# One stage for the return of the expert rows and the set-up of the graph layers, the far-sender table on ScalarE, the attention vectors in one pass per head

## The chip, the cores and the metric

The kernel runs on one core of a Trainium2 chip. The metric is the device time of one execution in microseconds (us), from the median of several runs. Engine names: PE is TensorE (PEld its weight loads), DVE is VectorE, ACT is ScalarE, POOL is GpSimd, SP is SyncE, which here only issues transfers. A name followed by q (PEq, POOLq, SPq) is that engine's sequencer.

## What is computed

There are N = 1250 nodes with D = 512 features each, and four layers, each of which adds its result to x. The change lies at the seam of the second and the third:

```python
x = x + _L0_gnn_ref(_layernorm(x), edge_attr_4, edge_attr_8, edge_index, ...)
x = x + _L0_ffn_ref(_layernorm(x)[None], ...)[0]        # experts, 2 of 4 groups, 2 of 8 in each
x = x + _L1_gnn_ref(_layernorm(x), edge_index, ...)     # two attention layers and a matrix
x = x + _L1_ffn_ref(_layernorm(x)[None], ...)[0]

def _L0_ffn_ref(inp, ...):          # per group g
    moe = moe + iw[:, e:e + 1] * (h @ W2[g, e] + b2[g, e])
    y = _layernorm(z + moe, gln_g[g], gln_b[g])
    out = out + gw[:, g:g + 1] * y

def gat_conv(x, src, dst, W, att_src, att_dst, bias):
    h = (x @ W).reshape(N, HEADS, HID)
    a_src, a_dst = jnp.sum(h * att_src, axis=-1), jnp.sum(h * att_dst, axis=-1)
    e = jax.nn.leaky_relu(a_src[src] + a_dst[dst], NEG_SLOPE)
    m = jax.ops.segment_max(e, dst, num_segments=N)
    e = jnp.exp(e - m[dst])
    ...
```

## The kernel before, in words

The nodes are cut into T = 10 tiles of P = 125. Work is staged: each `nc.Block()` is a stage with its own program on each engine, written out by hand with semaphores, and a stage begins when every engine has ended the one before (a barrier). There is no planner: an engine's order is the order of its lines.

**`routed_experts` (L1071)** has three stages. The first (planning, DVE above all) finds for each node its four experts, their gates (`wide`, `chosen_gate`) and the rows of `slot_rows` in which the results will lie (`slots`). POOL first clears `small` (L1183), then makes the constants on which DVE waits at L1225; SP loads the small tables and the first weights. The second stage runs 70 blocks of 128 rows through their experts and stores them to `slot_rows` in DRAM. The third (L1558 to L1690) is **the return**. POOL clears `wide_t` (L1562) and gathers, for every tile, four rows per node (`yg`, L1567; YB = 3 tiles deep). PE turns `wide` (L1584) and then for each tile makes `offsets` (L1593, two products), `sums` (L1600, L1601) and `gains` (L1608, two). On DVE `mix(t)` (L1644 to L1663) weighs and adds the rows and takes their statistics, `finish(t)` (L1670 to L1681) scales and adds them into `out`, which is x; the loop is `mix(t + 1)`, `finish(t)`. ACT takes the square roots (L1632). SP stores each finished tile (L1575).

**`graph_setup` (L1699)** is the next stage. On DVE it first normalises all ten tiles of x (`Norm`: L771, L774, L787, L791), and then for each tile subtracts two runs of the table `counts` (L1770), adds the identity (L1774) and writes `far` (L1776), which is -1e30 where a node sends to a receiver nothing and 0 elsewhere. Between tiles 2 to 5 it calls `attention_vectors` (L1818), which for each 128 rows of W1 and each of two attention rows makes a product of 128x1024 (L1824) and sums it by head (L1826). PE turns x (L1787) and `counts` (L1796, ten transposes a tile); ACT copies both out of PSUM (L1806, L1812).

**`graph_attention` (L1830)** follows twice. Its start needs `xt`, `wa`, `cnt` and `far`. In the first call `wa` is there; in the second DVE makes it with `attention_vectors`, eight times, while PE multiplies the first three tiles (L1954); PE then needs it at L1964. The pass for the maximum (L2093) is a product-and-reduce instruction over 1250 elements with an accumulator read behind it.

```python
mix(0)                                  # return, DVE
for t in range(T):
    if t + 1 < T:
        mix(t + 1)
    finish(t)
```

Of the kernel before, what the change touches and what calls it, by code (L numbers as in the profile page):

```python
# [4 lines left out]
F32 = mybir.dt.float32  # L5
F32R = mybir.dt.float32r
I32 = mybir.dt.int32
# [8 lines left out]
N = 1250  # L16
# [1043 lines left out]
J = TOP * TOP  # L1060
BLOCKS = (N * J + X * 127) // 128
# [9 lines left out]
def routed_experts(nc, queue, lg, z, weights, b2, gln_g, gln_b, z_rows, slot_rows, out, spare, x_new):  # L1071
# [8 lines left out]
    M = X + 2 * NG  # L1080
    ROWS = 128
    ctx = ExitStack()
    with ctx:
# [5 lines left out]

        chosen_gate = sb("chosen_gate", [P, J, T])  # L1090
        slots = sb("slots", [P, J, T], I32)
        wide = sb("wide", [P, T, TOP, M])
        ident = sb("ident", [128, 128])
        eps = sb("eps", [P, 1])
        small = sb("small", [ROWS, 3, D])
# [22 lines left out]
        with rooms:  # L1118
# [49 lines left out]
            with nc.Block() as block:  # L1168
                @block.sync
                def _(sp):  # L1170
                    sp.wait_ge(zeros, 1)
                    sp.dma_start(small[0:X, 0, :], b2.rearrange("g e d -> (g e) d")).then_inc(small_in, 16)
                    sp.dma_start(small[X:X + NG, 1, :], gln_g).then_inc(small_in, 16)
                    sp.dma_start(small[X + NG:M, 2, :], gln_b).then_inc(small_in, 16)
# [3 lines left out]
                    sp.wait_ge(small_in, 16 * 3)  # L1178
# [172 lines left out]
        with rooms:  # L1351
# [30 lines left out]
            with nc.Block() as block:  # L1382
                @block.sync
                def _(sp):
                    for e in range(X):
# [6 lines left out]
                        sp.sem_inc(ready, 1)  # L1392

                @block.gpsimd
                def _(pool):
# [143 lines left out]
        rooms = ExitStack()  # L1539
        with rooms:  # L1540
            def room(name, shape, dt=F32):
                return rooms.enter_context(nc.sbuf_tensor("p4_" + name, shape, dt))

            wide_t = room("wide_t", [ROWS, T * TOP, P])
            yg = room("yg", [P, YB, J, D])
            moe = room("moe", [P, 2, TOP, D])
            stats = room("stats", [P, 2, TOP, 6])
            mv = room("mv", [P, 2, TOP, 2])
            std = room("std", [P, 2, TOP])
            rstd = room("rstd", [P, 2, TOP])  # L1550
            psB, psG, psF = (ps[0:2], ps[2:4]), ps[4:6], ps[6:8]
            wide_mm, wide_ok, off_mm, moe_ok, sum_mm, gain_mm, scaled, out_ok, mv_ok, std_ok, kept = (sem(s) for s in (
                "wide_mm", "wide_ok", "off_mm", "moe_ok", "sum_mm", "gain_mm", "scaled", "out_ok", "mv_ok", "std_ok",
                "x_stored"))
            cleared = sem("cleared")
            back = queue["back"]
            CUT = 4 * P

            with nc.Block() as block:
                @block.gpsimd  # L1560
                def _(pool):
                    nc.gpsimd.memset(wide_t[:], 0.0).then_inc(cleared, 1)  # L1562
                    for t in range(T):
                        if t >= YB:
                            pool.wait_ge(moe_ok, t - YB + 1)
                        for j in range(J):
                            pool.indirect_dma_start(yg[:, t % YB, j, :], None, slot_rows,  # L1567
                                                    bass.IndirectOffsetOnAxis(ap=slots[:, j, t:t + 1], axis=0))\
                                .then_inc(back[t % YB], 16)

                @block.sync
                def _(sp):
                    for t in range(T):
                        sp.wait_ge(out_ok, t + 1)
                        sp.dma_start(x_new[t * P:(t + 1) * P, :], out[:, t, :]).then_inc(kept, 16)  # L1575
                    sp.wait_ge(kept, 16 * T)

                @block.tensor
                def _(pe):
                    for i in range(T * TOP // 4):  # L1580
                        if i >= 2:
                            pe.wait_ge(wide_ok, i - 1)
                        for c in range(4):
                            last = nc.tensor.transpose(psG[i % 2][0:M, c * P:(c + 1) * P],  # L1584
                                                       wide[:, (4 * i + c) // TOP, c % TOP, :], ident[0:P, 0:P])
                        last.then_inc(wide_mm, 1)
                    pe.wait_ge(wide_ok, T * TOP // 4)

                    def offsets(t):
                        if t >= 2:  # L1590
                            pe.wait_ge(moe_ok, t - 1)
                        for a in range(TOP):
# [1128 lines left out]
```

## Time and profile before

| | us |
|---|---|
| median of 3 runs | 2354.38 (2353.44 to 2356.39) |
| profiled execution, its own time | 2353.07 |
| its span, first to last instruction | 2351.4 |
| PE, DVE, ACT, POOL busy | 2003.0, 1513.0, 1118.3, 748.9 |
| mean granted clock of TensorE | 0.917 of full |

The profiled execution is the record of one run. Its rows give engine, source line, what is written and read, the number of instructions, and in brackets the idle time before them with what ended it. In windows each engine has its busy time and number of instructions; PEclk is the granted clock of TensorE as a share of 2.4 GHz, so 0.50 is 1.2 GHz. A product of f32 matrices shows as two MATMUL records. Ends of matmuls are modelled: where several follow one another the distance of their starts is the better measure.

### The profile page before, as it was taken

What the parts mean: (1) busy time and instruction counts of PE and PEld (TensorE: products, weight loads), DVE (VectorE), ACT (ScalarE), POOL (GpSimd) and SP (SyncE); (2) the same over time, 40 slices, a digit from 0 to 9 for tenths busy, and PEclk for the clock granted to TensorE, in tenths of its full rate; (3) what the DMA queues carried; (4) which work ended last, traced back from release to release, by engine and by line L of the source; (5) the groups of instructions that cost most, each with busy time, mean ns of one, the idle gap of its engine ahead of it and who ended that gap; (6) DMA issues with size and microseconds to landing.
All of it is one profiled execution on the core that took longest, in us unless ns stands there. A gap on an engine that the chain in (4) does not pass through costs nothing. (4 is left out here: it accounts for less than half of the span.)

```text
span 2351.4 us, 36494 instructions
## 1 busy us (share of the span) xinstructions
PE 2003.0 (85%) x11260; PEld 1288.4 (55%) x11261; DVE 1513.0 (64%) x2331; ACT 1118.3 (48%) x2278; POOL 748.9 (32%) x629
## 2 busy tenths in 40 slices
PE   5899999999997738999975497999999999980997
PEld 2444444444445727777732444777344777540997
DVE  1289999999995774333348865777763778428011
ACT  5777777777773404555510313666001676210332
POOL 4287777777770012444453000000000000000453
PEclk9989999999998957999988598999999999995998
DMA  5565555555551423788544313000012100221794
GB/s 160 168 170 157 154 155 154 153 154 152 155 155 53 95 85 129 268 261 265 174 129 132 96 43 115 22 22 1 18 43 81 64 22 1 104 100 46 221 277 94
DMA packets 200741, 285.12 MB, mean 121 GB/s; under 512 B 116698, under 2 KB 128677, under 8 KB 196543
## 3 DMA queue, kind: packets, MB, share of 16 engines
q0 software_dynamic: 98272, 142.08, 21.2%
q1 hardware_dynamic: 100158, 137.67, 19.0%
q10 hardware_dynamic: 2209, 4.07, 0.5%
q8 instruction: 56, 0.92, 0.2%
q14 instruction: 46, 0.38, 0.0%
HBM read 233.52 MB, written 49.84 MB: 121 GB/s over the span
## 5 line engine op out<-in xcount | busy, mean ns | idle before, releaser
L565 POOL DMA_INDIRECT p_s<-node_table,e_src_rows x320 | 454.5, 1420 | 147.4 <-issue 86.7
L2004 PE MATMUL g_psO<-g_h,g_ring 125*125 125x257 f32 x1600 | 372.4, 388 | 19.7 <-DVE g_ring L2136 10.3
L2004 PEld LDWEIGHTS g_psO<-g_h,g_ring 125*125 125x125 f32 x1600 | 296.6, 190 | 92.1 <-DVE g_stage L2130 26.6
L703 PE MATMUL p_psW<-e_w,p_hid 64*125 64x512 f32 x640 | 275.4, 654 | 50.2 <-ACT z L580 24.7
L622 DVE TENSOR_TENSOR g_b<-z,p_s 125x1536 f32<-125x1536 f32 x160 | 273.6, 1751 | 0.0
L711 PE MATMUL p_psM<-g_b 125*32 125x384 f32 x648 | 249.5, 533 | 11.0 <-DVE p_key L684 5.9
L580 ACT ACTIVATE z<-p_psW 125x512 f32<-125x512 f32 x320 | 187.2, 585 | 147.0 <-PE p_psW L703 139.0
L715 PE MATMUL p_psM<-g_b 125*32 125x256 f32 x648 | 218.8, 422 | 0.0
L714 PE MATMUL p_psM<-g_b 125*32 125x256 f32 x648 | 211.3, 410 | 0.0
L713 PE MATMUL p_psM<-g_b 125*32 125x256 f32 x648 | 193.8, 426 | 0.0
L585 ACT ACTIVATE p_of<-e_node_ids,z 125x314 bf16<-125x314 f16 x320 | 176.2, 551 | 6.8 <-PE p_psC L720 3.1
L2069 ACT ACTIVATE g_ring<-g_ring,g_ident 125x625 f32<-125x625 f32 x160 | 131.0, 819 | 85.3 <-DVE g_ring L2117 84.5
L703 PEld LDWEIGHTS p_psW<-e_w,p_hid 64*125 64x125 f32 x640 | 71.6, 185 | 181.2 <-ACT z L580 113.8
L2136 DVE SCALAR_TENSOR_TENSOR g_ring<-g_ring,g_cnt 125x625 f32<-125x625 f32 x160 | 128.7, 804 | 39.2 <-ACT g_ring L2069 39.1
L1954 PE MATMUL g_psO<-g_a,g_b 128*125 128x512 f32 x320 | 141.2, 603 | 2.1 <-PEq L1907 2.1
L2093 DVE CUSTOM_DVE_ANT_0 g_ring<-g_rb,g_far 125x1250 f32<-125x1250 f32 x80 | 110.7, 1453 | 49.7 <-DMA g_rb<-sender_rows 49.7
L60 POOL MEMSET p_ident<- 128x128 f32 x5 | 1.0, 206 | 434.2 <-POOLq L2669 368.1
L1438 PE MATMUL p_ps<-p_xt,p_first_own 128*128 128x128 f32 x1120 | 138.4, 277 | 0.0
L1399 POOL DMA_INDIRECT p_xg<-z_rows,p_node_at x70 | 71.1, 1016 | 210.8 <-DVE p_y L1535 154.4
L712 PE MATMUL p_psM<-g_b 125*32 125x128 f32 x648 | 135.9, 294 | 0.0
L1438 PEld LDWEIGHTS p_ps<-p_xt,p_first_own 128*128 128x128 f32 x1120 | 132.6, 194 | 0.5 <-issue 0.5
L1450 PE MATMUL p_ps<-p_second_own,p_ht 128*128 128x512 f32 x280 | 131.6, 593 | 0.0
(357 smaller groups left out, 3775.2 us busy)
## 6 DMA issues: line engine op xcount, KB each, us to landing
p_ring<-in_L_ffn_weights SPq DMA_DIRECT2D x32, 1025.0 KB
slot_rows<-p_y POOLq DMA_DIRECT2D x70, 256.0 KB
p_w1s<-in_L_ffn_w SPq DMA_DIRECT2D x16, 1024.0 KB
g_a<-in_L_ffn_w SPq DMA_DIRECT2D x16, 1024.0 KB
hidden<-g_b SPq DMA_DIRECT2D x40, 250.0 KB, 3.2
p_hid<-hidden SPq DMA_DIRECT2D x160, 62.5 KB
g_rb<-receiver_rows SPq DMA_DIRECT2D x16, 610.4 KB
p_s<-node_table,e_src_rows POOLq DMA_INDIRECT x320
```

Source lines behind the costliest of these rows:

```text
L565: pool.indirect_dma_start(s[:, g % 4, c, :, :].rearrange("p k u -> p (k u)"), None, node_table, bass.IndirectOffsetOnAxis(ap=src_rows[:, g ...
L580: nc.scalar.activation(w[:, b, c, :, :].rearrange("p k u -> p (k u)"), psW[c % 2][0:P, :], ACT.Copy).then_inc(w_ok, 1)
L585: nc.scalar.activation(of[:, b, c, :], node_ids[:], ACT.Sigmoid, scale=STEEP, bias=rise[:, bass.ds(g, 1), c:c + 1].rearrange("p o c -> p ( ...
L622: last = nc.vector.tensor_tensor(msg[:, b, :, q:q + 3, :], w[:, b, :, p:p + 1, :].broadcast_to([P, C, 3, MUL]), s[:, at, :, 1:4, :], ALU.mult)
L703: nc.tensor.matmul(psW[c % 2][0:P, :], hid[part, b, c // 2, :], w4[part, :], start=True, stop=True)\
L711: nc.tensor.matmul(psM[i][0:32, 0:3 * MUL], a, rows_[:, 0:3, :], start=begin, stop=end)
L713: nc.tensor.matmul(psM[i][64:96, 0:2 * MUL], own[1], rows_[:, 4:7:2, :], start=begin, stop=end)
L714: nc.tensor.matmul(psM[i][32:64, MUL:3 * MUL], own[0], rows_[:, 4:6, :], start=False, stop=end)
L715: last = nc.tensor.matmul(psM[i][96:128, 0:2 * MUL], own[2], rows_[:, 4:8:3, :], start=begin, stop=end)
L1438: last = nc.tensor.matmul(psH[u % 2][:, m * 128:(m + 1) * 128], w1s[u % 2][:, k, m * 128:(m + 1) * 128], xt[:, u % 2, k, :], start=k == 0, ...
L1954: last = nc.tensor.matmul(psO[0:P, 2 * (t % 2) + j, :], xt[:, k, t * P:(t + 1) * P], ws[:, k, j * 512:(j + 1) * 512], start=k == 0, stop=k ...
L2004: last = nc.tensor.matmul(psO[0:P, j, 0:HW], ring[:, i % RING, j * P:(j + 1) * P], h[:, s, hd, :], start=s == 0, stop=s == T - 1)
```

## The change

The third stage of `routed_experts` and `graph_setup` go, and one stage, `combine`, stands in their place. What the return needs from the planning lies in a free part of the room `g_b` (`for_combine`), so that it outlives `routed_experts`. In `combine` each tile goes through return, normalisation, turning and the difference of the counts before the next: the DVE loop is `mix(t + 1)`, `finish(t)` with the row statistics, `difference(t + 2)`, attention vectors (tiles 2 to 5), `norm(t)`. `psB`, `psF` and `psX` have one buffer where they had two, `psC` has two banks where it had six, `rows16` three buffers where it had two. `far` is written by ACT as relu(-1e30 * counts + 1e30), positive, and subtracted at the maximum. `attention_vectors` uses four product-and-reduce instructions of 256 elements with an accumulator read each, in place of one product and one reduction of 1024; this holds in both attention layers. `small` is cleared and loaded during the experts' blocks, not before planning. `wide_t` is no longer cleared.

```diff
 # routed_experts, planning
-                    nc.gpsimd.memset(small[:], 0.0).then_inc(zeros, 1)
-                    pool.wait_ge(zeros, 1)
                     identity(nc, pool, tick, ident[:])
...
 # routed_experts, blocks, POOL
                     for b in range(XB - 1):
                         gather(b)
+                    nc.gpsimd.memset(small, 0.0).then_inc(zeros, 1)
...
 # combine
+            def _(sp):
+                for t in range(RB):
+                    counts_in(t)
+                for i, row in enumerate((att_src, att_dst)):
+                    sp.dma_start(att[:, i, :], row.partition_broadcast(128)).then_inc(att_in, 16)
+                for k in range(KD):
+                    sp.dma_start(ws[:, k, :], w[k * 128:(k + 1) * 128, :]).then_inc(ws_in[k], 16)
+                for t in range(T):
+                    if t + RB < T:
+                        counts_in(t + RB)
+                    sp.wait_ge(out_ok, t + 1)
+                    sp.dma_start(x_new[t * P:(t + 1) * P, :], xs[:, t, :]).then_inc(kept, 16)
...
+                def offsets(t):
+                    pe.wait_ge(wide_ok, t * TOP // 4 + 1)
+                    if t:
+                        pe.wait_ge(moe_ok, t)
...
+                def sums(t):
+                    if t:
+                        pe.wait_ge(out_ok, t)
...
+                def gains(t):
+                    pe.wait_ge(wide_ok, TURNS)
+                    if t:
+                        pe.wait_ge(scaled, t)
...
+                def turn_counts(t):
+                    pe.wait_ge(looped, t + 1)
+                    for k, (a, b) in enumerate(PARTS):
+                        n = NPARTS * t + k
+                        if n >= 2:
+                            pe.wait_ge(cnt_ok, n - 1)
...
+                for t in range(T):
+                    sums(t)
+                    gains(t)
+                    if t + 2 < T:
+                        offsets(t + 2)
+                    if t:
+                        turn_rows(t - 1)
+                    if t + 2 < T:
+                        turn_counts(t + 2)
+                turn_rows(T - 1)
...
+                def take_counts(t):
+                    act.wait_ge(looped, t + 1)
+                    nc.scalar.activation(far[:, t, :], rows[:, t % 2, 0:N], ACT.Relu, bias=away[:], scale=FAR)\
+                      .then_inc(far_ok, 1)
...
+                for t in range(T):
+                    if t + 1 < T:
+                        roots(t + 1)
+                    row_root(t)
+                    if t:
+                        take_rows(t - 1)
+                    if t + 2 < T:
+                        take_counts(t + 2)
...
+                difference(0)
+                difference(1)
+                mix(0)
                 for t in range(T):
+                    if t + 1 < T:
+                        mix(t + 1)
+                    finish(t)
+                    if t + 2 < T:
+                        difference(t + 2)
+                    if 2 <= t < 2 + KD:
+                        v.wait_ge(att_in, 32)
+                        v.wait_ge(ws_in[t - 2], 16)
+                        attention_vectors(nc, v, wa_ok, ws, att, prod, wa, t - 2)
+                    norm(t)
...
 # attention_vectors
-        n = tick(nc.vector.tensor_tensor(prod[:, i, :], ws[:, k, :], att[:, i, :], ALU.mult))
-        tick.wait(n)
-        nc.vector.tensor_reduce(wa[:, k, i, :], prod[:, i, :].rearrange("p (h c) -> p h c", h=HEADS),
-                                AX.X, ALU.add).then_inc(wa_ok, 1)
+        for hd in range(HEADS):
+            own = slice(hd * HC_GAT, (hd + 1) * HC_GAT)
+            last = nc.vector.tensor_tensor_reduce(out=prod[:, i, own], in0=ws[:, k, own], in1=att[:, i, own], scale=1.0,
+                                                  scalar=0.0, op0=ALU.mult, op1=ALU.add, accum_out=wa[:, k, i, hd:hd + 1])
+        last.then_inc(wa_ok, 1)
```

The order of DVE before, in the middle of `graph_setup`: one tile's difference and far table (L1770 to L1776) between two calls of `attention_vectors`.

```order
L1824 TENSOR_TENSOR p_prod<-g_a,p_att 128x1024
L1826 TENSOR_REDUCE g_wa<-p_prod 128x4
L1770 TENSOR_TENSOR p_rows<-p_rows 125x1252
L1774 TENSOR_TENSOR p_rows<-p_rows,p_ident 125x125
L1776 TENSOR_SCALAR g_far<-p_rows 125x1250
```

And the order of DVE now, one round of the loop in `combine` behind its `mix(7)` (t = 6, without attention vectors): `finish(6)` from L1818, its row statistics (L1832, L1834), `difference(8)` (L1780, L1784), `norm(6)`. `p_moe` are the weighed rows, `g_b` holds x.

```order
L1818 SCALAR_TENSOR_TENSOR p_moe<-p_moe,p_mv,p_psG 125x512 x2
L1822 RECIPROCAL p_rstd<-p_std 125x2
L1826 SCALAR_TENSOR_TENSOR g_b<-p_moe,p_rstd,p_psF 125x512
L1829 SCALAR_TENSOR_TENSOR g_b<-p_moe,p_rstd,g_b 125x512
L1832 BN_STATS p_row_stats<-g_b 125x6
L1834 BN_AGGR p_row_mv<-p_row_stats 125x2
L1780 TENSOR_TENSOR p_rows<-p_rows 125x1252
L1784 TENSOR_TENSOR p_rows<-p_rows,p_ident 125x125
L1838 RECIPROCAL p_row_rstd<-p_row_std 125x1
L1842 TENSOR_SCALAR p_normed<-g_b,p_row_mv,p_row_rstd 125x512
```

The far table has left this engine, and the difference and the normalisation now stand between one tile's return and the next.

The order of PE before, at the end of the return and in all of `graph_setup`: the last tiles' `offsets` (L1593), `sums`, `gains`, then all the transposes.

```order
L1600 MATMUL p_ps<-g_b,p_ident 125x512
L1601 MATMUL p_ps<-p_small,p_wide_t 125x512
L1608 MATMUL p_ps<-p_small,p_wide_t 125x512 x2
L1559 UNCONDITIONAL_BRANCH
L1779 UNCONDITIONAL_BRANCH
L1787 MATMUL p_psX<-p_ident,g_b 128x125 x40
L1796 MATMUL p_psC<-p_ident,p_rows 125x125 x100
```

And the order of PE now, from the end of one round of the loop in `combine` through the next.

```order
L1698 MATMUL p_psC<-p_ident,p_rows 125x125 x10
L1669 MATMUL p_psF<-g_b,p_ident 125x512
L1670 MATMUL p_psF<-g_b,p_wide_t 125x512
L1678 MATMUL p_psG<-g_b,p_wide_t 125x512 x2
L1662 MATMUL p_psB<-g_b,p_wide_t 125x512 x2
L1687 MATMUL p_psX<-p_ident,p_normed 128x125 x4
```

The transposes of the counts (L1698) now stand ahead of the sums and the gains (L1669 to L1678) of the next tile, for which DVE waits in `finish`.

## Rows read from the trace of the kernel before

**Rows 1.** The page's head.
```profile
span 2351.4 us, 36494 instructions
```

**Rows 2.** Windows: from:to, length, busy per engine, PEclk, DMA share, GB/s.
```profile
1208.60:1284.70 76.10, 53.15 (x111) 20.73 (x109) 70.32 (x130) 2.96 (x10) 43.35 (x34) 0.95 0.51 150
1284.70:1289.70 5.00, 0.00 (x0) 0.00 (x0) 0.00 (x0) 0.00 (x0) 0.02 (x1) 0.50 0.17 51
1289.70:1350.30 60.60, 27.77 (x134) 23.85 (x135) 55.40 (x77) 18.16 (x38) 0.52 (x3) 0.58 0.34 104
1350.30:1353.60 3.30, 1.62 (x9) 1.36 (x9) 0.00 (x0) 1.34 (x3) 0.07 (x1) 0.50 0.00 0
```

**Rows 3.** Timeline of DVE, one tile of the return: start, us, instruction.
```profile
1221.91 1.41 DVE L1644 SCALAR_TENSOR_TENSOR p_moe<-p_yg,p_chosen_gate,p_ps 125x512 f32<-125x512 f32 x2
1225.96 1.39 DVE L1670 SCALAR_TENSOR_TENSOR p_moe<-p_moe,p_mv,p_ps 125x512 f32<-125x512 f32 x2
1229.13 1.41 DVE L1644 SCALAR_TENSOR_TENSOR p_moe<-p_yg,p_chosen_gate,p_ps 125x512 f32<-125x512 f32 x2
```

**Rows 4.** Timeline of DVE in graph_setup, difference, far, attention vectors.
```profile
1313.29 1.45 DVE L1770 TENSOR_TENSOR p_rows<-p_rows 125x1252 f32<-125x1252 uint16 x1
1315.11 0.81 DVE L1776 TENSOR_SCALAR g_far<-p_rows 125x1250 bf16<-125x1250 f32 x1
1315.83 1.22 DVE L1824 TENSOR_TENSOR p_prod<-g_a,p_att 128x1024 f32<-128x1024 f32 x1
1318.22 1.22 DVE L1824 TENSOR_TENSOR p_prod<-g_a,p_att 128x1024 f32<-128x1024 f32 x1
```

**Rows 5.** Timeline of DVE in the first attention layer, product-and-reduce.
```profile
1374.26 1.46 DVE L2093 CUSTOM_DVE_ANT_0 g_ring<-g_rb,g_far 125x1250 f32<-125x1250 f32 x1
1375.64 1.46 DVE L2093 CUSTOM_DVE_ANT_0 g_ring<-g_rb,g_far 125x1250 f32<-125x1250 f32 x1
```

**Rows 6.** Groups of instructions by line in 1280 to 1560 us.
```profile
L2136 DVE SCALAR_TENSOR_TENSOR g_ring<-g_ring,g_cnt 125x625 f32<-125x625 f32 x46 | 37.0, 804 | 9.2 <-ACT g_ring L2069 9.2
L2117 DVE SCALAR_TENSOR_TENSOR g_ring<-g_rb,g_as_low,g_lines 125x625 f32<-125x625 f32 x24 | 20.9, 870 | 27.0 <-ACT g_lines L2059 18.7 <-PE g_psO L2004 8.1
```

**Rows 7.** Groups of instructions by line in 1189 to 1354 us.
```profile
L1562 POOL MEMSET p_wide_t<- 128x2500 f32 x1 | 2.2, 2182 | 5.3 <-POOLq L1382 5.3
L771 DVE BATCH_NORM_STATS2 p_norm_stats<-g_b 125x6 f32<-125x512 f32 x10 | 6.0, 678 | 5.1 <-PEq L2664 5.1
L791 DVE TENSOR_SCALAR g_b<-g_b,p_norm_mv,p_norm_rstd 125x512 f32<-125x512 f32 x10 | 4.7, 543 | 0.0
L1812 ACT ACTIVATE g_cnt<-p_psC 125x500 uint16<-125x500 f32 (+1 forms) x30 | 13.3, 524 | 33.6 <-PE p_psC L1796 33.6
```

**Rows 8.** Waits: engine line <- releaser: us in total, times, longest.
```profile
DVE p_moe L1644 <- DMA p_yg<-slot_rows,p_slots: 20.5, 2, 18.5
SPq L1559 <- DMA x<-g_b: 3.6, 1, 3.6
```

**Rows 9.** Timeline of PE in the return and in graph_setup.
```profile
1223.47 1.88 PE L1593 MATMUL p_ps<-p_small,p_wide_t 128*125 128x512 f32 x4
1315.13 2.46 PE L1796 MATMUL p_psC<-p_ident,p_rows 125*125 125x125 f32 x10 [7.24 <-DVE p_rows L1774]
```

**Rows 10.** Windows of 4 us, columns as in Rows 2.
```profile
1220.00:1224.00 4.00, 3.82 (x6) 1.77 (x7) 3.80 (x8) 0.00 (x0) 3.09 (x4) 0.60 0.64 179
1304.00:1308.00 4.00, 3.74 (x31) 3.14 (x29) 2.78 (x4) 3.15 (x7) 0.00 (x0) 1.00 0.33 132
1312.00:1316.00 4.00, 0.87 (x4) 0.88 (x5) 3.90 (x6) 0.00 (x0) 0.00 (x0) 0.50 0.11 30
```

**Rows 11.** Timeline of ACT, a copy of 1024 elements.
```profile
1169.54 1.06 ACT L1492 ACTIVATE p_second_own<-p_ring 128x1024 f32 x1
```

**Rows 12.** Timeline of DVE in the planning stage.
```profile
850.59 3.49 DVE L1225 TENSOR_TENSOR p_ties<-p_ties,p_earlier 125x3200 f32<-125x3200 f32 x1 [1.97 <-POOL p_nodes L1206]
```

**Rows 13.** Timeline of PE in the second attention layer.
```profile
1698.42 16.95 PE L1964 MATMUL g_psX<-g_b,g_wa 128*8 128x512 f32 x48
```

More of the change, by code:

```diff
@@ L1060 @@
 J = TOP * TOP
+WIDE = X + 2 * NG
 BLOCKS = (N * J + X * 127) // 128
@@ L1068, with for_combine, routed_experts @@
 SLOTS = BLOCKS * 128
-def routed_experts(nc, queue, lg, z, weights, b2, gln_g, gln_b, z_rows, slot_rows, out, spare, x_new):
+def for_combine(spare):
+    at = X * X + 2 * J * T * X + T * (NG + 1) * NE
+    sizes = [T * TOP * WIDE, J * T, J * T]
+    parts = []
+    for size in sizes:
+        parts.append(spare[0:P, at:at + size])
+        at += size
+    return (parts[0].rearrange("p (t a m) -> p t a m", t=T, a=TOP), parts[1].rearrange("p (j t) -> p j t", j=J),
+            parts[2].bitcast(I32).rearrange("p (j t) -> p j t", j=J),
+            spare[0:WIDE, 0:3 * D].rearrange("p (k d) -> p k d", k=3))
+def routed_experts(nc, queue, lg, z, weights, b2, gln_g, gln_b, z_rows, slot_rows, out, spare):
     H = 256
@@ L1696, with combine @@
 TH = T // 2
-def graph_setup(nc, xs, counts, xt, cnt, far, w, ws, att_src, att_dst, wa):
+def combine(nc, queue, spare, xs, slot_rows, x_new, counts, xt, cnt, far, w, ws, att_src, att_dst, wa):
     ctx = ExitStack()
@@ L1750, in _ @@
                 tick(nc.gpsimd.memset(eps[:], EPS))
+                tick(nc.gpsimd.memset(away[:], -FAR))
+                for t in range(T):
+                    if t >= YB:
+                        pool.wait_ge(moe_ok, t - YB + 1)
+                    for j in range(J):
+                        pool.indirect_dma_start(yg[:, t % YB, j, :], None, slot_rows,
+                                                bass.IndirectOffsetOnAxis(ap=slots[:, j, t:t + 1], axis=0))\
+                            .then_inc(back[t % YB], 16)
@@ L1752, in _ @@
             @block.vector
             def _(v):
[L1754 to L1765 removed]
+                tick = Ticks(v, sem("mixed"))
@@ new lines, in finish @@
+                def finish(t):
+                    s = t % 2
+                    v.wait_ge(gain_mm, t + 1)
+                    v.wait_ge(mv_ok, t + 1)
+                    for a in range(TOP):
+                        last = nc.vector.scalar_tensor_tensor(moe[:, s, a, :], moe[:, s, a, :], mv[:, s, a, 0:1],
+                                                              psG[0:P, a, :], ALU.subtract, ALU.mult)
+                    last.then_inc(scaled, 1)
+                    v.wait_ge(std_ok, t + 1)
+                    r = tick(nc.vector.reciprocal(rstd[:, s, :], std[:, s, :]))
+                    tick.wait(r)
+                    v.wait_ge(scaled, t + 1)
+                    v.wait_ge(sum_mm, t + 1)
+                    m = tick(nc.vector.scalar_tensor_tensor(xs[:, t, :], moe[:, s, 0, :], rstd[:, s, 0:1],
+                                                            psF[0:P, :], ALU.mult, ALU.add))
+                    tick.wait(m)
+                    nc.vector.scalar_tensor_tensor(xs[:, t, :], moe[:, s, 1, :], rstd[:, s, 1:2], xs[:, t, :],
+                                                   ALU.mult, ALU.add).then_inc(out_ok, 1)
+                    v.wait_ge(out_ok, t + 1)
+                    n = tick(nc.vector.bn_stats(row_stats[:, t, :], xs[:, t, :]))
+                    tick.wait(n)
+                    nc.vector.bn_aggr(row_mv[:, t, :], row_stats[:, t, :]).then_inc(row_mv_ok, 1)
@@ L2156, in graph_layers @@
           nc.sbuf_tensor("g_wa", [128, KL, 2, HEADS], F32) as wa):
-        graph_setup(nc, view(b, T, D)[0:P], counts, view(a, KD, N), cnt, far, w1, view(a, KD, DH, at=KD * N), as1, ad1, wa[:, 0:KD, :, :])
+        combine(nc, queue, spare, view(b, T, D)[0:P], slot_rows, x, counts, view(a, KD, N), cnt, far, w1,
+                view(a, KD, DH, at=KD * N), as1, ad1, wa[:, 0:KD, :, :])
         with nc.sbuf_tensor("g_h", [P, T, HEADS, HW], F32) as h:
```

394 lines of the change are left out of this document (166 added, 228 removed).

## The prediction

> **What bounds the kernel now.** I read the stages by window first. The return ends at 1284.7 us, nothing runs for 5.0, `graph_setup` has DVE until 1350.3, and 3.3 later the first attention layer begins [rows 2]. In the return DVE is busy 70.3 of 76.1, in `graph_setup` 55.4 of 60.6 [rows 2]. So DVE is the bound of the whole stretch of 145.0 us, and what counts is DVE's work, the idle stretch between the stages, and the waits that the new order gives DVE. The waits say what starts the stretch: the first tile's gathers, for which DVE waits 18.5, and 2.0 more for the second [rows 8]. The timelines then give the price of each piece.
>
> **What goes.** The gap of 5.0 [rows 2], of which 3.6 is the wait for the last store of x [rows 8]. It moves behind work: the last store now goes out while the last tile is normalised and turned, which takes longer than 3.6. The rest of that gap, 5.0 - 3.6 = 1.4, holds the end of `routed_experts` with its clearing of semaphores; I put 1.0 of it at the one boundary that is left. Far goes from DVE: 1315.83 - 1315.11 = 0.72 a tile, 7.2 in all [rows 4]. Two of the ten differences now run in the wait for the first gathers, 1315.11 - 1313.29 = 1.82 each [rows 4], 3.6 together. In planning DVE waits 1.97 for POOL's constants [rows 12], and POOL starts with a clearing of 1536 columns; at the pace of `wide_t`, 2500 in 2.18 [rows 7], that is 1.35 less for DVE to wait. I take -1.4.
>
> **The attention vectors.** One product and one reduction of 1024 take 1318.22 - 1315.83 = 2.39 [rows 4], eight times 19.1. Now there are 32 short product-and-reduce instructions. The long one has a pitch of 1375.64 - 1374.26 = 1.38 for 1250 elements, with its accumulator read in it [rows 5]. At 0.96 elements a ns, which the bare 1250 / 1.30 would need, some 0.08 is fixed, so one of 256 takes 0.27 + 0.08 = 0.35, and 32 take 11.1. Bounds: 0.28 by proportion (9.0), 0.50 if its fixed part doesn't overlap (16). I take 11.1, since the long ones did overlap. Both sources are f32 here, where the row's far table is bf16. The nearest pair for that is a three-operand instruction with two f32 sources in SBUF, 870 ns for 625 elements, against one with an f32 and a uint16 source, 804 [rows 6]: 8% more, not twice. The Trainium skill, "Vector Engine (DVE) Microarchitecture Reference", section "Points that are easy to get wrong", says that the scalar-tensor-tensor shape with two non-bf16 SBUF sources halves throughput; by that a short one would take about 0.61, and the saving here would be gone.
>
> In the second attention layer the same edit is worth nothing: PE goes from the first three tiles into the product with `wa` with no idle time [rows 13], so it and not DVE sets that start. The cover is those three tiles; it is gone only if the 64 short instructions take longer than the 16 pairs, 38.2, that is over 0.60 each.
>
> **The new stage, DVE from the first mix.**
> - Start. Before, POOL cleared `wide_t` for 2.18 [rows 7] ahead of the first gather; now it makes the constants, some 0.7. With 1.0 for the boundary the gathers start 0.5 earlier: 1208.6 becomes 1208. Now 3.9 MB of counts, attention rows and W1 are asked for in the same moments. I add 1 here and 2 at the second tile. (The sizes are the code's: three tiles of counts at 0.31, two rows to 128 partitions at 0.52, W1 at 2.1.) Bounds: 0 if the queues don't disturb each other; +14 if these bytes went wholly ahead, since 179 GB/s at a share of 0.64 [rows 10] mean some 280 at most.
> - Mix and finish: 1229.13 - 1221.91 = 7.22 a tile [rows 3], 72.2.
> - Row statistics and their aggregation, now one by one behind the row that they need: 0.68 [rows 7] and 0.2, 9.0 for ten tiles.
> - Normalisation: 0.54 [rows 7] and a reciprocal of one column, 0.75 a tile, 7.5.
> - Eight differences at 1.82 [rows 4]: 14.5. Attention vectors: 11.1. **DVE's work is 114.3.**
>
> **What DVE waits for now.** The gathers of the second tile, 1.9 as before and 2 more: 4. In the last two tiles the root on ACT and the last `gains` have nothing before them: 2.3.
>
> The new wait is for `gains`. PE turns the counts of tile t + 2 ahead of `sums` and `gains` of tile t + 1, and can't start before DVE's difference. From its end: at full clock ten transposes take half of 2.46 [rows 9], but their third part needs a bank that ACT empties behind the far table. That is 1250 elements on ACT, 1.3 by 1.06 for 1024 [rows 11], and 0.52 for the copy [rows 7], so PE is done after 2.2. Four passes take at most 1.88 at full clock [rows 9], sums and gains together 3.5. So `gains` stand 5.7 after the difference. DVE needs them after normalisation (0.75) and `mix` (1225.96 - 1221.91 = 4.05 [rows 3]), at 4.8. That is 0.9 of wait in the four counted tiles without attention vectors; in the other four the vectors (2.8) cover it. At half clock the same path is 2.6 + 7.0 = 9.6, a wait of 4.8, and 2.0 behind the vectors. So 3.6 in all at full clock, 27 at half. What clock? PE has 6 products of 512 and 14 transposes a tile, 5.2 + 1.7 of 12 to 13.5, nearly 60%; the return had 0.95 of clock at 53.2 of 76.1, `graph_setup` 0.58 at 27.8 of 60.6 [rows 2]. This lies between, nearer the first, and a low clock makes PE denser. In the return too it was down once, 0.60 from 1220 to 1224 [rows 10], and came back. I take **6**.
>
> Transposes count for the clock here: from 1304 to 1308 PE did nothing else and had 1.00, while the short bursts from 1312 had 0.50 [rows 10]. The Trainium skill, "TensorE: Matmul & The Clock Gate", "Part 4: PE-mode transpose", says that the full clock does not engage for transposes. The trace disagrees with that; were it so, the fourteen transposes would count as idle, and the third rival would be likelier.
>
> - Tail: four transposes, one copy of 500 elements on ACT (0.5 [rows 7]) and the barrier, 2.2 (3.3 before [rows 2]).
>
> **The sum.** 1209 + 114.3 + 4 + 2.3 + 6 + 2.2 = 1337.8, against 1353.6: -15.8. With planning -1.4 the profiled execution goes from 2353.07 to 2335.9; its span of 2351.4 [rows 1] lies 1.7 below its time, both move alike. The median is 1.3 higher, so I predict **2337** for it. As a check from the other side: 4.0 of the gap, 7.2 of far, 3.6 of differences, 8.0 of vectors, 1.1 of tail and 5.2 of DVE's idle time in `graph_setup` (60.6 - 55.4) go, 29.1; 6 for `gains`, 3 for gathers and some 4 for instructions that now run one by one come, which leaves 16.
>
> **Rivals.**
> 1. *The gathers starve.* The transfers for the set-up sit on SP's queue beside the gathers. If those get a third of the DMA for the 3.9 MB, the first tile comes 4 later and the second 5 more than I took: some 2343. For it: 3.9 MB are 14 us of a full DMA, and the return alone took 0.51 of it [rows 2]. Against: POOL itself issues no faster than it did, and the first mix needs only 1 MB. Chance 0.12.
> 2. *Short product-and-reduce instructions are slow.* At 0.61 each, the 32 cost 19.5 instead of 11.1, +8.4, and the 64 in the second layer 39.0 against 38.2, +1: 2346. Against it the pair of rows 6. At 0.70 the whole gain would be gone. Chance 0.13.
> 3. *The clock stays low, and PE's order becomes the bound.* This ends slower. The cycle is then difference, counts, sums, gains (9.6), `finish` (1229.13 - 1225.96 = 3.17), statistics 0.9, difference 1.8: 15.5 a tile, 124 for eight, where I have 12.1 four times and 13.5 four times, 102; +22, and 3 more in each of the last two: 2365. It decides from about 0.6 of the stage at half clock. For it: `graph_setup` sat at 0.50 with a third of PE busy. Against: at 15.5 PE would be busy nine tenths, which released the clock wherever it happened. Chance 0.06.
> 4. *All waits are covered*, the gathers undisturbed, the clock full: 6 + 3 less, some 2328. Chance 0.12.
>
> **How the numbers follow.** My forecast, 2331 to 2343, has 0.57. A measurement of this kernel tells 0.2%, 4.7 us, from no change: faster means below 2349.7. Rival 2 reaches that only at its worst, rival 3 never. Faster 0.89, same 0.05, slower 0.06. The range for 8 in 10 goes from rival 4 to rival 2 and over it: 2326 to 2348.
>
> **What would show it.** In the changed profile: one idle stretch between the experts' blocks and the attention layer; its end about 16 earlier; far on ACT at 1.3; short product-and-reduce pitch near 0.35; DVE waiting for `gains` about 1 to 2 in tiles 1, 2, 7, 8 and hardly in 3 to 6; PEclk over 0.85; PE at the second layer's `wa` with no idle time. I am wrong if DVE idles over 15 in the stage, or if the pitch is over 0.5.

## The result, and the profile after

The changed kernel takes **2371.45 us**, median of 4 runs (2367.52 to 2372.42), against 2354.41 for the kernel before (4 runs): ratio 1.0079, 95% interval 1.0063 to 1.0094. It is slower by 0.8%, where 0.7% faster was forecast, and it lies outside the range. The profiled execution took 2367.52.

The page's head and clock row, after. The slices are 59 us each; the new stage lies in slices 21 to 23, where PE is 5, 8 and 8 tenths busy and its clock at 6, 6 and 5 tenths.
```profile
span 2365.7 us, 36678 instructions
PE   5898999999996839999958897999999999990997
PEclk9989999999998857999966598999999999995998
```

I count from the end of the experts' last block, 1190.08 before and 1189.71 after, to the first PE row of the attention layer. That **stretch** took 1353.57 - 1190.08 = 163.5 before [rows 2] and 1365.08 - 1189.71 = 175.4 after. Windows of after: from the first mix to the last, from there to DVE's end, the tail, and the start of the attention layer.
```profile
1220.31:1337.47 117.16, 95.13 (x211) 45.62 (x212) 96.42 (x224) 31.61 (x57) 33.66 (x28) 0.60 0.40 113
1337.47:1362.83 25.36, 18.72 (x33) 7.60 (x32) 13.27 (x27) 4.04 (x9) 0.00 (x0) 0.50 0.05 16
1362.83:1365.08 2.25, 1.09 (x5) 0.74 (x5) 0.00 (x0) 0.59 (x1) 0.04 (x1) 0.50 0.17 64
1365.08:1384.99 19.91, 19.91 (x53) 6.92 (x54) 0.00 (x1) 2.84 (x6) 0.60 (x4) 0.89 0.11 36
```
DVE's work is what was forecast: in the 142.5 us from the first mix to its end its waits sum to 30 (20.4 for `gains`, 8.7 for the second tile's gathers, 1.1 for small ones), which leaves 112 with the short gaps between instructions, where 114.3 was forecast. PE is busy 95 of 117 at a clock of 0.60, where the return had 0.95 [rows 2]. The rest is waits. DVE's in the stage, after (compare [rows 8]):
```profile
DVE p_moe L1818 <- PE p_psG L1678: 20.4, 6, 5.4
DVE p_moe L1792 <- DMA p_yg<-slot_rows,g_b: 18.5, 2, 9.8
DVE p_rows L1780 <- DMA p_rows<-counts: 17.3, 2, 11.9
```
The first row is the wait for `gains`. The other two are the start: the counts and gathers of the first tiles. The DMA view from 1189.71 to 1225 us, after (last number: us from issue to landing), and of before from 1190 to 1215:
```profile
q1 hardware_dynamic: 1216, 3.96, 42.3%
q0 software_dynamic: 2331, 2.90, 36.3%
g_a<-in_L_gnn_W SPq DMA_DIRECT2D x4, 512.0 KB, 26.1
p_yg<-slot_rows,g_b POOLq DMA_INDIRECT x14, 15.6
```
```profile
q0 software_dynamic: 2209, 2.66, 36.5%
p_yg<-slot_rows,p_slots POOLq DMA_INDIRECT x11, 4.4
```
And the window over the worst of it, after: a DMA share above one, all engines full.
```profile
1200.00:1220.00 20.00, 6.84 (x26) 3.67 (x24) 3.50 (x4) 5.58 (x8) 14.27 (x11) 0.59 1.05 251
```
POOL issues the gathers as early as forecast (first constants at 1196.35), but a gather lands after 15.6 us instead of 4.4. The first mix comes 30.6 us behind the experts' end, before it was 18.5. The Trainium skill, "DMA: Bandwidth & Descriptors", section "Queues, rings and completion order", says that each DMA engine takes turns between the queues that have work for it; the two shares above, 42 and 36%, fit that, but no run here shows the turns themselves.

How `gains` come late is seen on PE. Rows of its timeline, after: from the counts to `gains` in one tile, and the same for the last `gains`.
```profile
1323.73 2.67 PE L1698 MATMUL p_psC<-p_ident,p_rows 125*125 125x125 f32 x10 [2.23 <-DVE p_rows L1784]
1326.19 1.92 PE L1669 MATMUL p_psF<-g_b,p_ident 125*125 125x512 f32 x2
1328.04 1.33 PE L1670 MATMUL p_psF<-g_b,p_wide_t 40*125 40x512 f32 x2
1329.20 1.88 PE L1678 MATMUL p_psG<-g_b,p_wide_t 40*125 40x512 f32 x4
1336.88 2.66 PE L1698 MATMUL p_psC<-p_ident,p_rows 125*125 125x125 f32 x10 [2.31 <-DVE p_rows L1784]
1339.34 1.91 PE L1669 MATMUL p_psF<-g_b,p_ident 125*125 125x512 f32 x2
1341.18 2.07 PE L1670 MATMUL p_psF<-g_b,p_wide_t 40*125 40x512 f32 x2
1343.05 3.61 PE L1678 MATMUL p_psG<-g_b,p_wide_t 40*125 40x512 f32 x4
```
From the end of DVE's difference to the end of `gains` it is 7.4 in the first and 9.8 in the second, which runs wholly at half clock (forecast: 5.7 at full, 9.6 at half). DVE's side:
```profile
1331.12 1.41 DVE L1818 SCALAR_TENSOR_TENSOR p_moe<-p_moe,p_mv,p_psG 125x512 f32<-125x512 f32 x2 [2.67 <-PE p_psG L1678]
1346.70 1.41 DVE L1818 SCALAR_TENSOR_TENSOR p_moe<-p_moe,p_mv,p_psG 125x512 f32<-125x512 f32 x2 [5.09 <-PE p_psG L1678]
```
What stays odd is the clock: PE is busy 81% of the time here, and in the return 70% went with 0.95 [rows 2]. One thing about its products is new, and the description of the change doesn't name it: `small` and `wide_t` are 40 rows deep (the rows over which a product sums) and no longer 128.

### The profile page after: what moved, and what is told of

It reads as the page before. It is cut to its first block and busy times, and to the rows that moved or that the text cites. A ratio compares the mean times of both kernels' runs of the same rounds, so it can differ in the third digit from the quotient of the medians.

```text
span 2365.7 us, 36678 instructions
## 1 busy us (share of the span) xinstructions
PE 2038.6 (86%) x11260; PEld 1300.8 (55%) x11261; DVE 1484.0 (63%) x2474; ACT 1134.3 (48%) x2297; POOL 752.7 (32%) x629
## 5 line engine op out<-in xcount | busy, mean ns | idle before, releaser
L565 POOL DMA_INDIRECT p_s<-node_table,e_src_rows x320 | 459.8, 1437 | 141.9 <-issue 88.8
L580 ACT ACTIVATE z<-p_psW 125x512 f32<-125x512 f32 x320 | 187.1, 585 | 147.7 <-PE p_psW L703 135.5
L715 PE MATMUL p_psM<-g_b 125*32 125x256 f32 x648 | 221.6, 427 | 0.0
L714 PE MATMUL p_psM<-g_b 125*32 125x256 f32 x648 | 213.3, 414 | 0.0
L713 PE MATMUL p_psM<-g_b 125*32 125x256 f32 x648 | 196.4, 431 | 0.0
```

The source lines that it names most:

```text
L565: pool.indirect_dma_start(s[:, g % 4, c, :, :].rearrange("p k u -> p (k u)"), None, node_table, bass.IndirectOffsetOnAxis(ap=src_rows[:, g ...
L580: nc.scalar.activation(w[:, b, c, :, :].rearrange("p k u -> p (k u)"), psW[c % 2][0:P, :], ACT.Copy).then_inc(w_ok, 1)
L713: nc.tensor.matmul(psM[i][64:96, 0:2 * MUL], own[1], rows_[:, 4:7:2, :], start=begin, stop=end)
L714: nc.tensor.matmul(psM[i][32:64, MUL:3 * MUL], own[0], rows_[:, 4:6, :], start=False, stop=end)
L715: last = nc.tensor.matmul(psM[i][96:128, 0:2 * MUL], own[2], rows_[:, 4:8:3, :], start=begin, stop=end)
```

## The experiments

The theories. **K**: the start is late because 3.9 MB for the set-up fill the DMA engines. **G**: `gains` are late because PE turns the counts ahead of them. **R**: the products of 40 rows hold the clock down. Rival to R, **P**: the pattern of dense and idle moments in the new order does it. All ran in four groups (1 to 4, 5 to 8, 9 to 12, 13 and 14), each with its own runs of the kernel before (medians 2344.3 to 2352.7), so only ratios compare. A ratio is the time over that of the kernel before. "+26.6" is a time behind the end of the experts' last block; before, the first mix is at +18.5 and the second at +24.6, and in the change at +30.6 and +43.5. The clock is that from the first mix to the last. Stretch, waits and clock come from one profiled execution each.

**1 (e1_late). Attention rows and W1 later.**
```
 for t in range(T):
     if t + RB < T: counts_in(t + RB)
+    if t == 0:
+        sp.wait_ge(moe_ok, 2)
+        ...the att and ws transfers, which stood ahead of the loop
```


> The changed kernel, but SP asks for the attention rows and W1 (3.1 MB) only once the second tile's rows have been weighed (moe_ok 2), not at the start of the stage. Theory K: the two first waits for gathers (9.8 and 8.7 us in the changed kernel, first mix at 1220.3 and not at 1208) come from these transfers standing beside the gathers. Then the first mix starts near 1209, the second waits 2 to 4, and the whole is 12 to 16 us below the changed kernel (about 2356). Rival: the gathers are late for a reason of their own (rows not yet stored, POOL slower), then both waits stay and the time stays within 3 us of 2371.

Measured: 2349.09, ratio 1.0024 (1.0014 to 1.0033), stretch 167.7. First mix at +26.6, where about +19 was expected, second at +33.3 instead of +43.5. K holds, for a third of the first mix's delay and half of the second's: 1.2 MB of counts still travel beside the gathers, which land after 6.9.

**2 (e2_order). PE's order.** 
```
-turn_counts(1)
 for t in range(T):
     sums(t)
     gains(t)
+    if t + 1 < T: turn_counts(t + 1)
     if t + 2 < T: offsets(t + 2)
     if t: turn_rows(t - 1)
-    if t + 2 < T: turn_counts(t + 2)
```

> The changed kernel with one edit on PE: the counts of a tile are turned behind the next sums and gains, not ahead of them. Theory G: the 20.4 us that DVE waits for gains come from this order at a low clock. Then they fall to 6 to 9 (the last tile's 5.4 stays, since nothing stands before it), and the time falls by 11 to 14, to about 2358. Rival: PE is simply full at half clock (13.9 us a tile), so that the wait only moves to the offsets or the counts: less than 4 us.

Measured: 2347.15, ratio 1.0008 (0.9996 to 1.0020), stretch 166.1. The waits for `gains` halve, 20.4 to 10.5, a little less than expected; PE is busy 108 of 115 and its clock is 0.56. So G holds. That PE is busier doesn't bring the clock, which speaks against P as long as the products are 40 deep.

**3 (e3_rows). Products 128 rows deep again.** 
```
-wide_t = sb("wide_t", [WIDE, T * TOP, P])
+wide_t = sb("wide_t", [128, T * TOP, P])
-spare[0:WIDE, 0:3 * D]          # small
+spare[0:128, 0:3 * D]
+nc.vector.memset(wide_t[:], 0.0).then_inc(cleared, 1)
```

> The changed kernel, but the products with wide_t and small are 128 rows deep again (the lower rows zero, cleared by DVE in its first wait) and not 40. Theory R: TensorE's granted clock fell (0.62 in the stage at 0.82 busy, where the return before had 0.95 at 0.70) because products 40 rows deep count for less. Then PEclk in the stage is over 0.85, the waits for gains fall from 20.4 to under 9, and the time falls by 12 or more. Theory P: the clock fell because of the order of work (transposes and idle stretches), then PEclk stays near 0.6 and the time within 3 us.

Measured: 2352.76, ratio 1.0031 (1.0021 to 1.0042), stretch 170.0. The order of work is the change's; DVE clears `wide_t` (2.1 us) in its first wait. Windows from the first mix to the last, in this kernel, then in experiment 2:
```profile
1213.60:1331.29 117.69, 80.19 (x211) 43.99 (x212) 96.75 (x224) 31.42 (x57) 33.72 (x28) 0.76 0.40 113
```
```profile
1211.22:1326.28 115.06, 108.03 (x205) 46.89 (x206) 96.45 (x225) 30.14 (x55) 33.67 (x28) 0.56 0.41 115
```
PE is less busy than in 2 and has more clock, 0.76. Depth counts, but the result lies between the two expectations: over 0.85, waits for `gains` under 9 and 12 us off were expected of R, and the waits are 14.9 and the stretch is 5.4 shorter. Experiments 10 and 11 show that the order of work has a share too.

**4 (e4_before40). The kernel before with products 40 rows deep**, nothing else, in `offsets`, `sums` and `gains`:
```
-wide_t[0:ROWS, TOP * t + a, :], small[0:ROWS, 1, :]
+wide_t[0:M, TOP * t + a, :], small[0:M, 1, :]
```

> The kernel before with one edit: its products in the return are 40 rows deep and not 128 (the same numbers, the lower rows were zero). Theory R: PEclk in the return falls from 0.95 to near 0.5 to 0.6, PE needs 10.4 us a tile at half clock where DVE needs 7.2, and the kernel gets 15 to 30 us slower. Theory P: PEclk stays at 0.95 and the time within 2 us of before.

Measured: 2372.41, ratio **1.0115** (1.0098 to 1.0132), the stretch 192.7 instead of 163.5. Its return, first mix to last, then the same window of the kernel before, then two rows of its PE:
```profile
1199.97:1287.52 87.55, 87.55 (x99) 28.96 (x97) 61.07 (x112) 2.66 (x9) 40.73 (x34) 0.50 0.44 124
```
```profile
1208.60:1272.49 63.89, 47.61 (x103) 18.92 (x102) 60.32 (x112) 2.66 (x9) 43.35 (x34) 0.97 0.59 170
```
```profile
1239.72 1.06 PE L1608 MATMUL p_ps<-p_small,p_wide_t 40*125 40x512 f32 x1
1240.58 3.62 PE L1593 MATMUL p_ps<-p_small,p_wide_t 40*125 40x512 f32 x4
```
PE never idles in 87.55 us, and the granted clock is 0.50 throughout. The same products with 88 rows of zeros below them had 0.97. R is shown, in the old order, with no transpose in that window: five of six products (512 columns, two records each) are 40 deep, one of six 125.

**5 (e5_all). The three edits together.**

> The changed kernel with three edits at once: attention rows and W1 asked for only after the second moe tile is ready; PE turns the counts of a tile behind the next sums; the products 128 rows deep. Alone each took 7.7, 9.3 and 5.4 us off the changed kernel's stretch from the experts' end to the attention layer's first PE row (175.4 to 167.7, 166.1, 170.0). Theory A (three separate causes: full DMA, order of PE's queue, clock held low by shallow products): they add, stretch 153 to 156, ratio to before 0.995 to 0.997. Theory B (one cause, the waits for the gains, which each edit shortens and which only go once): the gain stops where DVE has no wait for gains left, stretch 158 to 164, ratio 0.998 to 1.001. In both the first mix stays about 26 us behind the experts' end, since the counts' 1.2 MB are still asked for beside the gathers.

Measured: **2330.09**, ratio **0.9936** (0.9922 to 0.9949), stretch 147.1. Window from the first mix to the last, and DVE's waits:
```profile
1206.16:1307.01 100.85, 72.13 (x216) 36.03 (x217) 96.13 (x224) 31.05 (x57) 34.45 (x29) 0.90 0.54 151
```
```profile
DVE p_moe L1795 <- DMA p_yg<-slot_rows,g_b: 7.5, 1, 7.5
DVE p_moe L1821 <- PE p_psG L1681: 4.0, 1, 4.0
```
The first mix is at +25.7. Stretch and ratio lie below what A allowed, and B falls: the clock went up to 0.90, and the waits for `gains` sank to one. But that the three together give more than their sum is not shown. The stretch is 28.3 less than in the change's first profile, where the three alone gave 7.7, 9.3 and 5.4, 22.4 in all; against its second profile (177.3, experiment 12) it is 30.2 less, and the three alone make 28.1. By the ratios, with 1.0074 for the change, the three alone took 0.50, 0.66 and 0.43%, 1.59 in all, and together 1.38.

**6 (e6_start). The counts only after the first tile's gathers**, and DVE's first mix ahead of its first difference. On top of 5:
```
+sp.wait_ge(back[0], 16 * J)
 for t in range(RB): counts_in(t)
...
-difference(0)
-difference(1)
 mix(0)
+difference(0)
```
PE, ACT and DVE then take the counts one tile later throughout.

> As e5_all, and the counts are asked for only after the first tile's gathers have landed; DVE does the first mix ahead of the first difference. Theory A (the lost 12 us at the start are the gathers' turn in full DMA engines): first mix at +18.5 to +20 as in the kernel before (+18.5) instead of +26 to +31, the gathers' median time to landing back at 5 to 6 us, and the stretch 5 to 8 us shorter than in e5_all; ratio to before 0.991 to 0.995. Rival (it is queue issue on POOL or the cleanup ahead of them that is late, not the engines being full): first mix stays above +24.

Measured: 2335.4, ratio 0.9950 (0.9935 to 0.9966), stretch 150.6. The first mix is at +18.5, as before the change: K is shown for it; the gathers land after 6.0. But the stretch doesn't fall, it is 3.5 longer than in 5. DVE waits 15.0 for gathers where 5 has 7.5, the second mix is at +28.6, 3.7 ahead of 5 and no longer 7.2, and the clock is 0.83.

**7 (e7_oldvec). Attention vectors as before**, in both layers.
```
-for hd in range(HEADS): ... tensor_tensor_reduce(out=prod[:, i, own], ...)
+nc.vector.tensor_tensor(prod[:, i, :], ws[:, k, :], att[:, i, :], ALU.mult).then_inc(pr_ok, 1)
+v.wait_ge(pr_ok, 2 * k + i + 1)
+nc.vector.tensor_reduce(wa[:, k, i, :], ..., AX.X, ALU.add).then_inc(wa_ok, 1)
```

> The changed kernel with the attention vectors as before (a product of the whole row, then a reduction, with a wait between) in both graph layers. If they lie on the path, DVE's work in the stage grows by 16 passes of about 1.2 us against 32 of 0.345: 8 us longer, ratio about 1.011 to 1.012. If half the tiles that carry them wait for gains from PE anyway, part of it is hidden: 3 to 6 us longer, ratio 1.009 to 1.010. The second graph layer stays as it is within 0.5 us (its vectors are covered).

Measured: 2363.72, ratio 1.0077 (1.0059 to 1.0094), stretch 183.7, 8.4 longer than in the change's first profile. The time is not what either case expected. The change's second profile is in experiment 12.

**8 (e8_fardve). The far table by DVE.**
```
-nc.scalar.activation(far[:, t, :], rows[:, t % 2, 0:N], ACT.Relu, bias=away[:], scale=FAR)
+v.wait_ge(looped, t + 1)
+nc.vector.tensor_scalar(far[:, t, :], rows[:, t % 2, 0:N], 0.0, CAP, ALU.is_equal, ALU.mult)
```

> The changed kernel with the far-sender table again by DVE (tensor_scalar, eq and times a cap) and not by ScalarE. Theory A (DVE's own work bounds the stage): 10 passes of about 0.7 us more on DVE, 7 us longer, ratio about 1.011. Theory B (while PE's clock is low the chain PE, ACT, PE behind the gains bounds it, so DVE has room): within 2 us of the changed kernel, ratio 1.007 to 1.009, DVE's waits for gains shorter by what its own work grew.

Measured: 2360.93, ratio 1.0072 (1.0055 to 1.0090), stretch 177.1; DVE's busy time from first to last mix rises from 96.4 to 103.0, its waits for `gains` sink from 20.4 to 14.3. What ScalarE takes over was, in the changed kernel, given back as waiting: B.

**9 (e9_sep). The kernel before, stages apart, with only the far table by ScalarE and the new vectors.** The edits of 7 and 8 the other way round, in `graph_setup`; ScalarE takes far(t) ahead of the copies of tile t.

> The kernel before, its two stages left apart, with only the two other parts of the change: far-sender table by ScalarE and attention vectors in one pass per head. In the setup of the graph layers they take 16 passes of 1.22 us off DVE for 32 of 0.345 (8.5 us) and 10 of 0.81 us (8.1, the last of which was beside PE's transposes). If DVE alone bounds that part: 15 to 16 us shorter, stretch 148, ratio 0.993 to 0.994. If in the six tiles without attention vectors the counts (two buffers, 1.0 us of wait in two tiles before), PE at half clock (2.5 us a tile) and ScalarE (1.33 + 1.34 us a tile) take over: 11 to 13 us shorter, stretch 151 to 153, ratio 0.9945 to 0.9955. Either would say that the joining itself brings nothing beyond these two parts.

Measured: 2341.09, ratio **0.9959** (0.9945 to 0.9973), stretch 152.2, the second of the two cases. ScalarE's copies now wait 7.0 for PE and PE 13.9 for DVE in the set-up. Two of the three parts of the change are worth 0.4%; the third, the joining as it was made, costs 1.0074 / 0.9959, about 1.2%.

**10 (e10_late_rows) and 11 (e11_order_rows). Two of the three edits of 5**: late transfers and deep products (10), order and deep products (11).

> Of e5_all's three edits only two: the late attention rows and W1, and products 128 rows deep; PE keeps the changed kernel's order. Additive from the single runs: stretch 175.4 - 7.7 - 5.4 = 162, ratio about 1.000. If the clock is what multiplies them (it was 0.60 and 0.76 with one edit, 0.90 with three), it stands at 0.8 or more between first and last mix and the stretch is 153 to 158, ratio 0.996 to 0.998.

> Of e5_all's three edits only two: PE's counts behind the next sums, and products 128 rows deep; attention rows and W1 are asked for at the stage's start as in the change, so first and second mix stay at +30 and +44. Additive: stretch 175.4 - 9.3 - 5.4 = 160.7, ratio about 0.999. If the clock multiplies them: clock 0.85 or more, stretch 155 to 158, ratio 0.996 to 0.998.

Measured: 10: 2347.76, ratio 0.9987 (0.9977 to 0.9997), stretch 159.9, clock 0.76. 11: 2346.75, ratio 0.9985 (0.9973 to 0.9996), stretch 157.9, clock 0.86. The stretches lie 2 to 3 below the sums; against the change's second profile the sums are 160.4 and 158.8, and they lie only 0.5 and 0.9 below; the ratios show nothing of it. So 10 is in effect additive, and its clock stayed under the 0.8 of the other case; 11 reached the clock and the stretch of the other case, but not its ratio. With products 128 deep the order of the change has 0.76 (3 and 10) and the new order 0.86, so P has a share beside R. Only order and depth together bring the clock over 0.8. The rest of the waits for `gains` is then 4.4, against 16.8 in 10.

**12 (after_again). The changed kernel again.**

> The changed kernel on the chip of the experiments, as their base: ratio to before 1.005 to 1.008, stretch 174 to 177, clock about 0.60 between first and last mix.

Measured: 2367.84, ratio 1.0074 (1.0056 to 1.0091), stretch 177.3, clock 0.60. So the slowdown is found again. Against it, 7 and 8 are the same within their intervals. Their stretches say +6.5 and -0.2, but one execution each, and the change's own two differ by 1.9. So in the changed kernel the far table by ScalarE shows no gain, and whether the new vectors are worth something there stays open.

**13 (e12_one) and 14 (e13_spread). The start once more.** 13 asks for only the first tile's counts at once; 14 also spreads W1's four pieces over three tiles. On top of 5:
```
+counts_in(0)
+sp.wait_ge(back[0], 16 * J)
-for t in range(RB): counts_in(t)
+for t in range(1, RB): counts_in(t)
...
 difference(0)
-difference(1)
 mix(0)
+difference(1)
```

> e5_all, with only the first tile's counts asked for at the stage's start and the others once the first tile's gathers have landed; DVE's second difference moved behind the first mix. If the late start is a term of its own: first mix at +19 to +20, stretch 142 to 146, ratio 0.991 to 0.992. If the wait comes back at the second tile's gathers (beside which the counts now travel) or in a lower clock: stretch 148 to 151, ratio 0.993 to 0.994.

> e12_one, with W1's four pieces asked for one tile after the other (from the second tile on) and not together. If the gathers of the second and third tiles waited for W1's 2 MB: 2 to 4 us shorter than e12_one, wait for gathers under 5 us in all. If not: within 1 us of it.

Measured: 13: 2337.63, ratio 0.9934 (0.9915 to 0.9953), stretch 150.4, first mix +18.7. 14: 2335.53, ratio 0.9931 (0.9909 to 0.9953), stretch 145.9 in its profile, which its time doesn't bear out. None is told apart from 5. Waits of 13:
```profile
DVE p_rows L1785 <- DMA p_rows<-counts: 11.7, 3, 5.9
DVE p_moe L1797 <- DMA p_yg<-slot_rows,g_b: 6.1, 2, 5.0
DVE p_moe L1823 <- PE p_psG L1683: 4.4, 1, 4.4
```
The wait goes from the first tile's gathers to the second tile's counts. In 5, 13 and 14 DVE waits 20 to 25 us in all for the cleanup, counts and gathers; the order of the transfers shifts that between them and hardly lessens it.

The best versions, 5, 13 and 14, are faster than both kernels, by 0.65% against before and 1.4% against the change.

## Why the prediction was wrong

Two steps failed: the gathers at the start were priced by POOL's pace and not by full DMA engines, and the clock was taken from PE's share of busy time, without the new depth of its products. By its own sign, DVE idle over 15 in the stage, it was wrong: 30 us of waits from the first mix on. By its steps, in the profiled execution, forecast start of the attention layer 1337.8, measured 1365.1, 27.3 later:

- **The start failed**: "I add 1 here and 2 at the second tile". The first mix came at 1220.3, not 1209: **+11.3**. The wait of the second tile was 8.7, not 4: **+4.7**. The bound of +14 was worked out and then not believed; I argued from POOL's pace of issue, while the engines, full, set the pace of landing. Experiments 1 and 6 show it. Rival 1 was this mechanism and had 0.12, at half its size. What this term costs in the end is less plain than where it stands: where the first mix came back to +18.5 (6, 13, 14), DVE waited later instead.
- **The wait for `gains` failed, by its clock**: 6 and 2.3 for the last tiles were forecast, and 20.4 and 1.1 measured, **+13.2**. The path was right (9.8 at half clock against 9.6 worked out; 5.1 of wait against 4.8). Between 0.95 and 0.58, "nearer the first", was wrong: 0.60. The argument took the clock as a matter of PE's share of busy time alone, and "at 15.5 PE would be busy nine tenths, which released the clock wherever it happened" was the sentence that kept rival 3 at 0.06. In experiment 4 PE is busy ten tenths and the clock stays at 0.50. The trace of before has no products 40 deep; the full diff makes them so, and I had not costed that edit. It is the step that is missing.
- **Rival 3** named the mechanism and the sign, 2365 for 2371, though not for that reason, and the cycle never became PE's alone.
- **Planning failed, -1.4**: it gained nothing (below).
- **DVE's work was right**: 112 for 114.3, **-2.1**. The four numbers make 11.3 + 4.7 + 13.2 - 2.1 = 27.1 of the 27.3. Vectors: pitch 0.345 for 0.35, rows beneath; the 0.61 of rival 2 is not what this instruction takes. In the second layer nothing moved, as forecast: PE goes on with the product with `wa` with no idle time. Far on ACT 1.33; one idle stretch; tail 2.25 for 2.2.

Timeline of DVE, attention vectors after, then PE at the second layer's `wa`:
```profile
1268.54 0.42 DVE L1870 CUSTOM_DVE_ANT_0 p_prod<-g_a,p_att 128x256 f32<-128x256 f32 x1
1268.88 0.42 DVE L1870 CUSTOM_DVE_ANT_0 p_prod<-g_a,p_att 128x256 f32<-128x256 f32 x1
```
```profile
1698.69 13.04 PE L1999 MATMUL g_psO<-g_a,g_b 128*125 128x512 f32 x30
1711.66 0.60 PE L2009 MATMUL g_psX<-g_b,g_wa 128*8 128x512 f32 x1
```

The remaining 2 to 3 us of the slowdown lie behind the stretch: the second layer's product with `wa` moved by 13.2, the stretch's end by 11.5. The first part of the first attention layer, 53 records on PE, ran at 0.89 of clock and took 19.91, where before it had 0.93 and took 19.30; why the rest was lost was not tried.

With three edits the joined kernel comes to the time that was forecast: experiment 5's ratio of 0.9936 is 2339 of 2354.4. In part that is luck. Its stretch of 147.1 is near the 147.7 of the forecast (1337.8 - 1190.1), but the first mix comes at +25.7 and not at +18.9, and from there to DVE's end it takes 119.3 and not 126.6. And more than half of that gain (0.41 of 0.64%) comes from the other two parts, without the joining (experiment 9).

## What to carry to other kernels

Cutting a product's depth to the rows that hold data saves room and can cost half of TensorE's clock: look at granted clock and depth together, and pad with zeros where PE is near the bound. When a stage is pulled forward, its transfers come too: count the bytes that then stand beside the transfer that starts the stage, and take the bound from a full DMA, not from the issuing engine. In a joined stage, put on the in-order engine first what the bound engine waits for next, and only then the work that is merely ready.

## What the runs showed of the hardware

**Depth and clock.** 100% busy with five of six products 40 rows deep: granted clock 0.50 for 87.6 us. The same with 128 rows, 88 of them zeros: 0.95 to 0.97 at 70 to 75% busy. In the joined stage, 40 rows against 128: 0.60 against 0.76 with the change's order (after, 3 and 10), 0.56 against 0.86 to 0.90 with the other (2, 11 and 5). Transposes of 125 rows, some 14 a tile, don't stand in the way: from 1220 to 1240 experiment 5 had 1.00. Nor do shallow products that run side by side in different rows of the array. In the first layer of the kernel before PE runs nothing but products 16 and 64 rows deep for 23 us, and the granted clock is 1.00:
```profile
30.40:53.80 23.40, 23.40 (x148) 9.59 (x140) 0.00 (x0) 21.95 (x43) 0.00 (x0) 1.00 0.59 202
39.50 2.04 PE L364 MATMUL p_psH<-p_ea,p_w1q 16*128 16x500 f32 x8
41.47 2.31 PE L374 MATMUL p_psH<-p_h,p_w2h 64*64 64x500 f32 x16
```
Sixteen records of 500 columns in 2.31 us are side by side: four of 512 in a row take 1.88. So it is the product that runs alone in few rows that goes with the low clock here.

**POOL held by DVE.** The clearing of `small` is gone from planning and POOL starts its constants 1.4 us earlier against DVE's first comparison; yet DVE waits 1.97 as before [rows 12]. Timelines of DVE and POOL, after, and POOL's row before:
```profile
842.49 3.49 DVE L1222 TENSOR_TENSOR p_above<-g_b 125x3200 f32<-125x3200 f32 x1 [12.23 <-PEq L2701]
```
```profile
842.81 3.33 POOL L63 TENSOR_SCALAR_AFFINE_SELECT p_ident<-p_ident 128x128 f32<-128x128 f32 x1 [0.15 <-POOL p_ident L60]
1196.70 0.29 POOL L63 TENSOR_SCALAR_AFFINE_SELECT p_ident<-p_ident 128x128 f32<-128x128 f32 x1
```
```profile
842.91 1.89 POOL L63 TENSOR_SCALAR_AFFINE_SELECT p_ident<-p_ident 128x128 f32<-128x128 f32 x1 [0.15 <-POOL p_ident L60]
```
The same instruction takes 0.29 where DVE is idle (the second of after's rows). Beside DVE's first comparison it ends with it, at 846.1 for 842.49 + 3.49 = 846.0; before, at 844.8 for 844.7. So it had waited for DVE in both, and what POOL gained ahead of it was lost in it. The Trainium skill, "SBUF — State Buffer", section "SBUF: two separate sides", says that VectorE with two SBUF inputs and a GpSimd operation that reads SBUF hold a port pair by turns, each for its whole instruction; these rows agree with it.

**Gathers in full DMA engines.** Medians over the first 25 to 35 us: 4.4 us to landing alone, 6.9 beside 1.2 MB of other loads, 15.6 (24.1 at most) beside 3.9 MB.
